# A graph-attention layer on one core: GpSimd's pause awaits all but the last one or two gathers, gathers signal two lanes of semaphores, and 6 units are in flight, not 12

## What is computed

```python
q, k, v = x @ Wq + bq, x @ Wk + bk, x @ Wv + bv      # each (N, 4, 32)
attn = einsum('nhc,mhc->hnm', q, k) / sqrt(32)
alpha = softmax(where(adj == 0, -inf, attn), axis=-1)  # 0 where a row has no edge
out = einsum('hnm,mhc->nhc', alpha, v)
x_r = x @ Ws + bs
beta = sigmoid(concat([out, x_r, out - x_r]) @ Wb)
result = layernorm(x + beta * x_r + (1 - beta) * out)
```

## Time and profile before, and how to read them

| | us |
|---|---|
| median of 3 runs | 1977.79 |
| lowest and highest | 1976.16, 1981.87 |
| the profiled execution | 1964.78 |
| its span (first to last instruction) | 1962.9 |
| POOL busy in the span | 1174.4 (60%) |
| DVE busy | 1310.3 (67%) |
| PE busy | 1164.9 (59%) |
| ACT busy | 839.9 (43%) |

### The profile page before, as it was taken

One profiled execution on the slowest core, in us unless ns is written; L12 is line 12 of the kernel. 1 busy time (PEld: TensorE's weight loads), 2 busy tenths in 40 slices (PEclk: granted clock), 3 DMA queues, 4 the chain that ended last, 5 costly groups with the idle time before them and its releaser, 6 DMA issues.

```text
span 1962.9 us, 20126 instructions
## 1 busy us (share of the span) xinstructions
PE 1164.9 (59%) x4696; PEld 680.4 (35%) x4696; DVE 1310.3 (67%) x3389; ACT 839.9 (43%) x1595; POOL 1174.4 (60%) x1711
## 2 busy tenths in 40 slices
PE   7322746657574756466655657756766668444553
PEld 5101433334342334233323334423423334233342
DVE  5876878666756776557656468757555677886564
ACT  2331443334643463344634348545635476431112
POOL 4454565566566656656566656565665665676664
PEclk9565677677776776667777578876667767666565
DMA  9947856666755776564866668776767778433331
GB/s 334 354 164 199 318 198 233 214 233 223 293 197 183 258 271 234 216 218 161 342 230 215 247 243 294 265 258 247 252 217 278 249 255 280 140 89 96 94 89 57
DMA packets 130037, 438.70 MB, mean 223 GB/s; under 512 B 26567, under 2 KB 61198, under 8 KB 97150
## 3 DMA queue, kind: packets, MB, share of 16 engines
q1 hardware_dynamic: 76510, 297.15, 41.1%
q0 software_dynamic: 52832, 136.07, 22.5%
q10 hardware_dynamic: 576, 4.19, 0.5%
HBM read 417.93 MB, written 19.44 MB: 223 GB/s over the span
## 4 chain that ended last, share of the span: by engine, by line
POOL 34%; issue 24%; DVE 13%; DMA 13%; PE 7%; DVEq 4%; another core or an unknown queue 3%; ACT 2%; SPq 1%; ACTq 0%; POOLq 0%
POOL s_kv L799 31%; DMA s_kv<-kv_rows,s_rec_in 11%; DVE s_raw L1248 2%; DVE s_kv L1246 2%; PE s_acc L1001 1%; DVEq L1296 1%; DVE s_wtop L1295 1%; POOL node_records L766 1%; POOL out_rows L775 1%; ACT s_mask L1023 1%; DVEq L1443 1%; DVE s_kv L1272 1%; DVE s_d_max L1454 1%; PE s_ps_key L889 1%
## 5 line engine op out<-in xcount | busy, mean ns | idle before, releaser
L799 POOL DMA_INDIRECT s_kv<-kv_rows,s_rec_in x1023 | 1024.3, 1001 | 700.6 <-DMA s_kv<-kv_rows,s_rec_in 340.6
L829 PE MATMUL s_ps_w<-s_mask,s_bit_w 128*128 128x512 bf16 x1008 | 374.6, 521 | 332.4 <-ACT s_mask L1023 233.8
L1023 ACT ACTIVATE s_mask<-s_adj_in 128x2048 bf16<-128x2048 f32 x252 | 478.2, 1900 | 114.5 <-DMA s_adj_in<-in_adj 66.7
L1001 PE MATMUL s_acc<-s_kv,ident 128*128 128x128 f32 x2032 | 321.3, 330 | 109.9 <-DVE s_kv L1272 62.8
L1001 PEld LDWEIGHTS s_acc<-s_kv,ident 128*128 128x128 f32 x2032 | 312.2, 244 | 137.4 <-DVE s_kv L1272 77.3
L829 PEld LDWEIGHTS s_ps_w<-s_mask,s_bit_w 128*128 128x128 bf16 x1008 | 111.3, 120 | 559.1 <-ACT s_mask L1023 294.9
L1246 DVE TENSOR_TENSOR s_kv<-s_kv,s_ps_q 128x1536 f32<-128x1536 f32 (+15 forms) x76 | 147.1, 1935 | 235.2 <-DMA s_kv<-kv_rows,s_rec_in 224.3
L1272 DVE TENSOR_TENSOR s_kv<-s_kv,s_ps_q 128x1536 f32<-128x1536 f32 (+15 forms) x76 | 146.7, 1931 | 17.9 <-ACT s_ps_q L1062 10.1
L1062 ACT ACTIVATE s_ps_q<-s_sc 128x56 f32<-128x56 f32 (+17 forms) x76 | 16.7, 220 | 318.4 <-DVE s_sc L1262 218.5
L1248 DVE TENSOR_REDUCE s_raw<-s_kv 128x48 f32<-128x1536 f32 (+15 forms) x76 | 147.1, 1935 | 5.6
L1050 ACT COPY s_xs<-s_ps_x 128x128 f32<-128x128 f32 x63 | 16.6, 264 | 288.7 <-remote 160.4
(11 more groups left out here) (281 smaller groups left out, 1563.2 us busy)
## 6 DMA issues: line engine op xcount, KB each, us to landing
s_adj_in<-in_adj SPq DMA_DIRECT2D x248, 1024.0 KB
s_kv<-kv_rows,s_rec_in POOLq DMA_INDIRECT x1023
kv_rows<-s_kv SPq DMA_DIRECT2D x16, 512.0 KB, 7.6
s_rec_in<-node_records SPq DMA_DIRECT2D x55, 106.0 KB
s_kv<-in_x_cols SPq DMA_DIRECT2D x4, 1024.0 KB, 8.4
s_adj_in<-in_adj ACTq DMA_DIRECT2D x4, 1024.0 KB
s_d_in<-in_x_cols SPq DMA_DIRECT2D x8, 512.0 KB
s_d_v<-kv_rows SPq DMA_DIRECT2D x8, 512.0 KB
```

The source lines that it names most:

```text
L799: nc.gpsimd.indirect_dma_start(out=kv[0:n, START[k] + s], out_offset=None, in_=kv_dram[:, :], in_offset=bass.IndirectOffsetOnAxis(ap=rec_i ...
L829: last = nc.tensor.matmul(w[:], bit_w[:, slab], mask[:, k % 2, s * WORD:(s + 1) * WORD], start=False, stop=(slab == SLABS - 1))
L1001: last = nc.tensor.matmul(acc[:, c * D:(c + 1) * D], ident[:], kv[:, START[k] + s, D:2 * D], start=(s == 0), stop=(s == plain(k) - 1))
L1023: nc.scalar.activation(mask[:, q % 2], adj_in[:, q % ADJ_RING], ACT.Sign, accum_out=edges[:, t, h:h + 1]).then_inc(masked, 1)
```

## The change

The pause now stands before the count of gathers and awaits another one. Gathers are numbered through the whole program (`ORDER`) and taken in pairs. With g gathers issued, `pause_before` awaits the last gather of the last pair that is complete and has at least one gather behind it: one gather is left in flight when g is odd, two when g is even. Consecutive pairs signal two different lanes, so that the count awaited holds nothing from the gathers left in flight: each unit has two semaphores in place of one. That doubles the semaphores for a given FLIGHT, and FLIGHT is 6 in place of 12, so `FREE` uses 2 * (k + 1 - 6). DVE waits for both lanes of its unit.

```diff
-FLIGHT = 12
+FLIGHT = 6
...
+ORDER = [(k, s) for k in range(len(UNITS)) for s in range(HELD[k])]
+ORDER_OF = {ks: i for i, ks in enumerate(ORDER)}
+PAIR = 2
+
+
+def lane_of(k, s):
+    return ORDER_OF[k, s] // PAIR % 2
+
+
+def lane_landed(k, s, lane):
+    return 16 * sum(j % FLIGHT == k % FLIGHT and lane_of(j, i) == lane for j, i in ORDER[:ORDER_OF[k, s] + 1])
...
-def slots_landed(k):
-    return 16 * sum(s for j, s in enumerate(HELD[:k + 1]) if j % FLIGHT == k % FLIGHT)
...
-        gathered = [sem(f"gathered{i}") for i in range(FLIGHT)]
+        gathered = [[sem(f"gathered{i}_{lane}") for lane in range(2)] for i in range(FLIGHT)]
...
-            begun = {"since": 0, "last": None}
-
-            def pause_after(n):
-                if begun["since"] + n > RUN and begun["last"] is not None:
-                    k, s = begun["last"]
-                    pool.wait_ge(gathered[k % FLIGHT], slots_landed(k) - 16 * (HELD[k] - 1 - s))
-                    begun["since"] = 0
-                begun["since"] += n
+            run = {"transfers": 0, "gathers": 0}
+
+            def pause_before(n):
+                if run["transfers"] + n > RUN and run["gathers"] > PAIR:
+                    k, s = ORDER[(run["gathers"] - 1) // PAIR * PAIR - 1]
+                    pool.wait_ge(gathered[k % FLIGHT][lane_of(k, s)], lane_landed(k, s, lane_of(k, s)))
+                    run["transfers"] = 0
+                run["transfers"] += n
...
-                    pause_after(1)
-                    begun["last"] = (k, s)
+                    pause_before(1)
+                    run["gathers"] += 1
...
-                        bounds_check=last_row, oob_is_err=False).then_inc(gathered[k % FLIGHT], 16)
+                        bounds_check=last_row, oob_is_err=False).then_inc(gathered[k % FLIGHT][lane_of(k, s)], 16)
...
-                dve.wait_ge(gathered[k % FLIGHT], slots_landed(k))
+                for lane in range(2):
+                    dve.wait_ge(gathered[k % FLIGHT][lane], lane_landed(k, HELD[k] - 1, lane))
```

More of the change, by code:

```diff
@@ L750, in _ @@
             last_row = pool.to_reg(N)
-            begun = {"since": 0, "last": None}
-            def pause_after(n):
-                if begun["since"] + n > RUN and begun["last"] is not None:
-                    k, s = begun["last"]
-                    pool.wait_ge(gathered[k % FLIGHT], slots_landed(k) - 16 * (HELD[k] - 1 - s))
-                    begun["since"] = 0
-                begun["since"] += n
+            run = {"transfers": 0, "gathers": 0}
[5 more added lines that the diff above has]
+                run["transfers"] += n
             def scatter_records(w):
-                pause_after(len(WINDOWS[w]))
+                pause_before(len(WINDOWS[w]))
                 pool.wait_ge(x_placed[w], 16)
```

## The result

| | before | after |
|---|---|---|
| median, us | 1976.97 (1967.95 to 1981.87, 4 runs) | 1816.25 (1811.07 to 1820.85, 4 runs) |
| ratio | | 0.919, 95% interval 0.915 to 0.923 |
| the profiled execution, us | 1964.78 | 1820.85 |
| forecast for the median, us | | 1859 (range 1812 to 1925) |

The gain is 161 us between the medians. The forecast had 119 us, with the right mechanism and sign. The time lies in its range, 4 us inside the lower end. Most of the missing 42 us were gained in one stage, as will be seen.

A forecast was written before the change was run, and what follows sets the result against it. POOL was taken as the bound, by its 1.30 us per gather and its pauses, with DVE pacing some stages. Gains 103 + 23 + 7 less 10 and 4 made 119 us: 1977.8 - 119 = 1859 us, range 1812 to 1925.

The forecast's parts named there:

- The price of a pause: POOL's waits for landing gathers: 1.30 us shorter per gather left in flight, no wait below 0.30 us.
- the first two stages: 127 to 340 us and 340 to 1447 us: shorter pauses give 23 us of lead and 103 us.
- the 14 taken back: Costs of the change: 10 us of POOL waiting for slots, 4 us for one more DVE wait per unit.
- the third stage: 1447 to 1896 us: DVE and the chain behind it set the pace, shorter pauses worth almost nothing.
- DVE's waits to about 100: Sign in the changed kernel's profile: DVE's waits for gathers fall from 224 to about 100 us.
- POOL's waits for slots: POOL, with more lead, meets slots not yet free: 10 us lost, bounds nothing and 14 us.
- DVE's second wait: DVE issues one wait more per unit: 0.05 us each, 4 us lost, bounds 0 and 14 us.
- Last stage: From 1896 us to the end, POOL sets the pace: half of DVE's 15.4 us of waits gained, 7 us.
- The DMA rival: Saturated DMA engines set landings in loaded pauses, so only short pauses and the end pay: 1950 us, chance 0.12.
- The queue rival: POOL's queue lacks room for up to fourteen gathers, so its instructions wait: slower, 2051 us, chance 0.06.
- No change: POOL's waits move from pauses to slots, records or rows to be stored: 1978 us, chance 0.04.
- More than forecast: Gathers land 2 us apart under load, 139 + 34 in place of 103 + 23: 1812 us, chance 0.04.

The follow-up runs named there:

- the repeat: The kernel before, unchanged, executed once more for a second profile: 1972.05 us.
- the late-only kernel: The changed kernel with its pause only from unit 47 on, earlier pauses awaiting the last gather issued: 1925.02 us, ratio 0.976.
- PAIR = 6: The changed kernel with pauses that leave one to six gathers in flight: 2167.51 us, and 1708.95 us (0.867) when run again.
- PAIR = 4: The changed kernel with pauses that leave one to four gathers in flight: 1743.02 us (0.884), and 1742.88 us when run again.
- PAIR = 1: The changed kernel with every pause leaving exactly one gather in flight: 1867.61 us, ratio 0.947.

## Why the prediction was right, and where it was not

**The bound: right.** POOL's rate and its pauses set the pace, "issue" (0.31 us a gather, 295.5 us) and the 1.00 us of the gathers did not move, and most of what was taken off the pauses reached the end: of 169.5 us, DVE's waits lost 145 and the execution 151.

**The price of a pause: right in kind, a little high.** Forecast was 1.30 us per gather left, cut where a pause gets too short, for the first two stages 103 + 23 = 126 us. Over the whole program the change took 400.3 - 225.9 = 174 us off for 161 gathers left, 1.08 each. With one left in every pause it is 1.15. But no pause shows the price by itself, since pauses change their kind. Of the 56 pauses that took 3 us or more in the repeat, 35 still do in the changed kernel; on average these lost 0.75 us with one gather left (15 pauses) and 1.65 us with two (20), less than priced. The other 21 became short and lost 4.1 us each, more than leaving two gathers can bring. The other way round, of the 16 pauses under 3 us that leave one gather, seven got longer, up to 5.51 us. As the program around it gets faster, a pause meets the loads of adjacency at another moment. The one in front of the record scatters of unit 16 took 2.10 us before and 5.17 after. Here are the microseconds before its end in the windows view, in the repeat and then in the changed kernel; the last two numbers are the DMA engines' share and GB/s:

```profile
532.00:534.00 2.00, 2.00 (x11) 2.00 (x11) 1.69 (x9) 0.61 (x3) 0.00 (x0) 0.50 0.15 46
```

```profile
486.10:491.20 5.10, 4.35 (x14) 1.38 (x13) 4.30 (x17) 4.15 (x7) 0.00 (x1) 1.00 1.04 348
```

The first two stages became 15.4 and 92.7 us shorter, 108 us, against 126 minus the 14 taken back, 112. Calling the first stage DVE's was not quite right either: DVE waited 7.3 us for gathers there in the repeat, and the stage lost twice that.

**The step that failed: the third stage.** "From 1447 to 1896 us ... DVE and the chain behind it set the pace" rested on the earlier trace rows, 2.9 us of waits in 24 units, and so the pauses there were priced at nothing. They are worth 40 us in that stage, as the late-only kernel shows. By the prediction's own rule, the repeated profile of before would have come close: it has 25 pauses in that stage, 84.6 us in all, and 1.30 us for each gather left, with no pause under 0.30, makes some 46 us (an estimate, pause by pause), under a cap of 59.4 us of waits. The row was true of its execution, and no measure of what DVE was waiting for in others. This term is 40 us; the others together fell 6 us short of the forecast. The last 8 of the 42 us lie between single executions, whose stages add up to 152 us, and medians (161). The same profile fed the sign "DVE's waits to about 100".

**The small terms.** POOL's waits for slots were forecast to grow by 10 us. Against the kernel before (14.2 us, 13.7 in the repeat) they grew by 3 or 4, against the changed kernel with the old pause (6.8 us) by 10.5, so whether the term was too high is not settled. DVE's second wait was forecast at 4 us, which was too high, and FLIGHT = 6 at 0; the kernel with both and the old pause is 0.2% faster than before, so neither costs anything that can be measured. Last stage: 7 us forecast, 4.5 found.

**The range: held, in part by luck.** Its lower end, 1812 us, stood for landings 2 us apart, and a gather left was worth 1.08 us. What brought the time there was the third stage, which had no part in the range. And the two bounds do not follow from the counts given: with 38 loaded and 13 quiet pauses and 0.34 and 0.66 as shares, 1.0 us apart makes 83 us in place of 80, and 2.0 us apart makes 150 in place of 139, so that this end should have been some 10 us lower. The forecast itself, 103 us, is added up rightly.

**The DMA rival: wrong.** It gave 1950 us. With the loaded pauses in the majority, POOL's early return did bring the gathers earlier to DVE. The Trainium skill (DMA: Bandwidth & Descriptors, section on issuing engines not being separate DMA queues) says that starting transfers on several engines at once saves only the sequencer's time for starting them. No run here starts the gathers from a second engine, so none tests that. What the prediction drew from it, that under a burst an earlier issue brings DVE nothing, the measured time refutes: by the rival only the quiet pauses and the end would have paid, 28 us. Gathers in the middle of a burst were not followed by themselves.

**The queue rival: wrong**, as far as six gathers left, with up to 18 transfers issued past the one awaited. It decided from a mean of 1.12 us; the mean was 1.00 in every kernel. *No change* is refuted by the time. *More than forecast* came nearest to it with 1812 us, but its reason, landings 2 us apart, does not fit 1.08 us for each gather left. POOL's waits for landings came to 226 us where about 200 had been named as a sign. ACT waited 62.5 us for adjacency in the changed kernel and 73.0 in the repeat of before, so it did not become the bound.

**Why two lanes at all.** The Trainium skill (the same page, section on why a DMA increments its semaphore by 16) holds that with two transfers in flight on one semaphore the count can be reached before the first has wholly landed, as 16 engines finish on their own. No run here shows that. By it, leaving gathers in flight needs a second semaphore, and the runs show that the second one costs nothing that can be measured.

## What to carry to other kernels

Where an engine both issues transfers and sets the pace, as POOL does here, a wait for the last transfer issued costs what is left of its latency. Awaiting one a few places back cost nothing here and was worth 0.9 to 1.0 us for each gather left, somewhat under the issue interval of 1.30 us, until the pauses reached their floor. Before a stage is written off as bound by somebody else, look whether the profile can be trusted on it: "remote" in a program of one core and gathers without a time to landing were both in the profile before, and a second profile of the unchanged kernel cost one run. And repeat a surprising measurement beside a kernel whose time is known, before explaining it.

## What the runs showed of the hardware

- The same kernel (PAIR = 6) had medians of 2167.51 and 1708.95 us, four runs each, the first with 64% of its transfers' semaphore events missing from the one trace that was kept, and with waits of up to 45 us that only "remote" ends. The instructions were as fast as ever: DVE was busy 1309.5 us in the one and 1312.8 in the other. The kernel before, with half of its events missing, took 1964.78 us and is no slower for it. Which comes first, the missing events or the unexplained waits, what condition brings both, and whether it would be there without a profiler, stays open.
- The Trainium skill (DMA: Bandwidth & Descriptors, section on the anatomy of one DMA on the SWDGE path) gives a transfer some 2.0 us fixed plus its bytes; by its rate a gather of 128 KB would take 2.3 us, an estimate. The trace of the changed kernel tells the landing of only 262 of the 1023 gathers. Counted from the start of the issuing instruction, the fastest of them took 2.20 us, which fits, and the median 4.3 us, with the longest at 9.7: beside loads of 1 MB the figure is a floor and not a typical value. The quiet pause's 2.11 us is counted from the end of that instruction, 1 us later.
- Each gather left in flight took 1.04 to 1.15 us off the waits up to PAIR = 4, where gathers are issued 1.30 us apart. Pauses that took 3 us or more both in the repeat and in the kernel with PAIR = 1 (44 of them) lost 0.92 us; all 56 that did in the repeat lost 1.45. Between these two, how far apart gathers land under load stays open. Part of the shortfall is pauses that had little to lose, or that met a load they had not met before.
